# First attention in two passes of two batches, with the queries and keys of a head as seven half products

## The reference, cut to what matters

```python
projected = jnp.einsum('bsd,ed->bse', x, w_in)          # x is the layer norm here
q, k, v = jnp.split(projected.reshape(b, s, 16, 3 * 128), 3, axis=-1)
scores = jnp.einsum('bqhd,bkhd->bhqk', q, k) * (1.0 / np.sqrt(128))
scores = jnp.where(causal_mask, scores, -jnp.inf)
out = jnp.einsum('bhqk,bkhd->bqhd', jax.nn.softmax(scores), v)
return jnp.einsum('bse,de->bsd', out.reshape(b, s, 16 * 128), w_out)
```

## Time and profile before

| | whole span | 480 to 540 us (first attention) |
|---|---|---|
| PE busy | 2306.0 us (94%) | 60.00 of 60 us |
| DVE busy | 1661.4 us (68%) | 36.40 |
| ACT busy | 1120.8 us (46%) | 27.42 |
| POOL busy | 611.0 us (25%) | 9.98 |
| granted TensorE clock (1.00 is 2.4 GHz) | 0.983 | 1.00 |

### The profile page before, as it was taken

One profiled execution on the slowest core, in us unless ns is written; L12 is line 12 of the kernel. 1 busy time (PEld: TensorE's weight loads), 2 busy tenths in 40 slices (PEclk: granted clock), 3 DMA queues, 4 the chain that ended last, 5 costly groups with the idle time before them and its releaser, 6 DMA issues. The chain is left out here.

```text
span 2440.7 us, 40753 instructions
## 1 busy us (share of the span) xinstructions
PE 2306.0 (94%) x12966; PEld 1979.7 (81%) x12966; DVE 1661.4 (68%) x3852; ACT 1120.8 (46%) x2649; POOL 611.0 (25%) x497
## 2 busy tenths in 40 slices
PE   6999999999999999978999779999999999889997
PEld 5889898989898988856788558888888888767886
DVE  7555555564655554577666748998998999975666
ACT  3444444343434443443333435665666566542334
POOL 1111111110111111135121323333333333234223
PEclk9999999999999999989999889999999999999998
DMA  4524333334242424224885200000000000017866
GB/s 167 180 93 141 132 109 136 132 104 168 92 179 92 154 104 143 105 86 184 295 284 189 77 19 1 19 19 0 18 18 18 0 18 18 18 53 272 278 237 233
DMA packets 101006, 279.83 MB, mean 115 GB/s; under 512 B 8840, under 2 KB 11272, under 8 KB 95264
## 3 DMA queue, kind: packets, MB, share of 16 engines
q1 hardware_dynamic: 80032, 222.81, 25.9%
q0 software_dynamic: 11360, 37.76, 4.0%
q10 hardware_dynamic: 9504, 17.85, 2.2%
HBM read 133.40 MB, written 144.98 MB: 114 GB/s over the span
## 5 line engine op out<-in xcount | busy, mean ns | idle before, releaser
L74 PE MATMUL bank<-xT_hi,w_hi 128*128 128x512 f32 x864 | 349.7, 405 | 18.6 <-POOL w_lo L700 5.7
L76 PE MATMUL bank<-xT_hi,w_lo 128*128 128x512 f32 x864 | 343.3, 397 | 0.0
L75 PE MATMUL bank<-xT_lo,w_hi 128*128 128x512 f32 x864 | 343.3, 397 | 0.0
L619 DVE TENSOR_TENSOR hq_lo<-bank,hq_hi 128x512 fp32r<-128x512 f32 (+1 forms) x256 | 157.1, 624 | 251.5 <-ACT hq_hi L555 104.7
L609 DVE SCALAR_TENSOR_TENSOR x<-bank,inv,x 128x512 f32<-128x512 f32 x256 | 182.0, 748 | 170.6 <-PE bank L76 170.6
L74 PE MATMUL bank<-wo_hi,hq_hi 128*128 128x512 f32 x576 | 232.3, 403 | 15.3 <-DVE x L1050 13.7
L75 PE MATMUL bank<-wo_lo,hq_hi 128*128 128x512 f32 x576 | 226.7, 393 | 0.0
L76 PE MATMUL bank<-wo_hi,hq_lo 128*128 128x512 f32 x576 | 226.5, 393 | 0.0
L74 PEld LDWEIGHTS bank<-xT_hi,w_hi 128*128 128x128 f32 x864 | 166.2, 192 | 54.8 <-DVE xT_lo L178 9.8
L76 PEld LDWEIGHTS bank<-xT_hi,w_lo 128*128 128x128 f32 x864 | 165.5, 192 | 35.6
L75 PEld LDWEIGHTS bank<-xT_lo,w_hi 128*128 128x128 f32 x864 | 165.8, 192 | 33.9
(11 more groups left out here) (297 smaller groups left out, 6309.4 us busy)
## 6 DMA issues: line engine op xcount, KB each, us to landing
sorted_x<-blank SPq DMA_DIRECT2D x48, 1584.0 KB, 10.9
arena<-split_w SPq DMA_DIRECT2D x32, 1024.0 KB, 5.9
split_w<-arena SPq DMA_DIRECT2D x48, 512.0 KB, 3.0
raw<-dram_wr SPq DMA_DIRECT2D x24, 512.0 KB, 5.9
w_raw<-dram_wa SPq DMA_DIRECT2D x16, 512.0 KB, 3.8
arrived<-routed_y SPq DMA_DIRECT2D x8, 1024.0 KB, 8.2
w_raw<-dram_wb SPq DMA_DIRECT2D x8, 768.0 KB, 4.4
row_pt_hi<-sorted_x ACTq DMA_DIRECT2D x22, 264.0 KB, 4.2
```

Of the source, the lines that this page charges most:

```text
L74: nc.tensor.matmul(out, hi, mov_hi, start=first, stop=False)
L75: nc.tensor.matmul(out, hi, mov_lo, start=False, stop=False)
L76: return nc.tensor.matmul(out, lo, mov_hi, start=False, stop=last)
L619: return nc.vector.tensor_tensor(out, bank, hi.bitcast(F32), ALU.subtract).then_inc(done, 1)
```

## The change

The order becomes two passes: pass 0 does batches 0 and 1 for all 16 heads, pass 1 does batches 2 and 3. There are still 64 steps, now s = 2·(16·pass + head) + i. All weights are loaded and split in each pass, so twice.

For heads 1 to 14 of each pass the queries and keys of both batches are one 2x2 block product (batch x half of the features, times half of the features x query or key weights), done by Strassen's scheme in Winograd's form: seven half products (M1 to M7, each two k, 6 matmuls) and not eight. The operands that are sums are made beside: POOL sums weights (T1 to T4, four 128x256 operations per head, then split like weights), and once per pass, in head 0, POOL and DVE sum the inputs, stored where the other pair of batches has its xT. The results are summed by DVE out of PSUM, seven 128x512 operations per head, into SBUF buffers; the rounded part and the remainder of q and k are then taken from those buffers. Heads 0 and 15 keep whole queries and keys; head 0 holds the input sums, and head 15 holds the layer norm of the next pair of batches (pass 0: batches 2 and 3 for this attention; pass 1: batches 0 and 1 for the mixture of experts), whose tiles POOL scales. In pass 1 the statistics of batches 0 and 1 stand at the end of step i = 0 of head 14. The core of the diff, first the half product and one of its users, and PE's order in heads 1 to 14 (even i = 0, even i = 1, odd i = 0, odd i = 1) and in head 15:

```diff
+    def half_product(bank, weights, j, inputs, begin=True, close=True):
+        for k in range(2):
+            at = slice((2 * j + k) * DH, (2 * j + k + 1) * DH)
+            last = product(nc, m.bank[bank][:, :], weights[HI][:, at], weights[LO][:, at],
+                           inputs[HI][:, k, :], inputs[LO][:, k, :], begin and k == 0, close and k == 1)
+        return last
...
+    def m5(g, h):
+        pe.wait_ge(a.folded, folds_to(g, h, FOLD_U2))
...
+        half_product(4, m.wt, T1, sums(g, 1)).then_inc(a.folding, 1)
...
+        elif not edge(h) and not odd and i == 0:
+            m5(g, h)
+            outputs((0, 1))
+            m2(g, h)
+            turned()
+            m3(g, h)
+            outputs((2, 3))
+            attended()
...
+            project_v(g, h, i, 0)
...
+            project_v(g, h, i, 1)
+        elif not edge(h) and not odd:
...
+            m7(g, h)
+            outputs((0, 1))
...
+            m4(g, h)
+            turned()
+            outputs((2, 3))
+            pe.wait_ge(a.folded, folds_to(g, h, FOLD_Q1))
+            project_v(g, h, i, 0)
+            attended()
+            project_v(g, h, i, 1)
+        elif not edge(h) and i == 0:
+            pe.wait_ge(a.v_lo, values_count(g, h, odd, 1) - 2)
+            m1(g, h)
+            outputs((0, 1))
...
+            m6(g, h)
+            turned()
+            m5(g, h)
+            m2(g, h)
+            m3(g, h)
+            outputs((2, 3))
+            attended()
+        elif not edge(h):
+            m7(g, h)
+            outputs((0, 1))
+            m4(g, h)
+            turned()
+            outputs((2, 3))
...
+            m1(g, h + 1)
+            attended()
+            m6(g, h + 1)
...
+            norm_tiles(g, i, v, (0, 1))
+            whole_q(g, h, odd, i)
+            norm_tiles_out(g, i, (0, 1))
+            outputs((0, 1))
+            turned()
+            norm_tiles(g, i, v, (2, 3))
+            whole_k(g, h, odd, i)
+            attended()
+            norm_tiles_out(g, i, (2, 3))
+            outputs((2, 3))
```

ACT: odd heads, i = 0 (in front of it stand the late weights, the exponentials and `split_wo`), and the end of a step:

```diff
+            if odd:
+                first_product(g, h, s, 0)
...
+            probs_hi(u)
+            if odd:
+                query_hi(g, h, s, i)
+            key_hi(g, h, s, i)
...
+            if not odd and i:
+                sums_hi(g)
         if n1:
...
+            output_hi(u)
+        if new and not odd:
+            values_hi(g, h, i)
+        if new and i:
+            if g == 0:
+                prepare(h)
```

DVE, after `mask_and_max`: odd heads i = 0, heads 1 to 14 i = 1, the tail of head 0, and the end of a step:

```diff
+            add((0, 1))
+            with_m6(g, h, s)
+            probs_lo(u, (0,))
+            with_m5(g, h, s)
+            probs_lo(u, (1, 2))
+            first_query(g, h, s)
+            first_key(g, h, s)
+            query_lo(g, h, s, i)
+            key_lo(g, h, s, i)
+            add((2, 3))
...
+            second_key(g, h, s)
+            add((0, 1))
+            second_query(g, h, s)
+            probs_lo(u)
+            key_lo(g, h, s, i)
+            query_lo(g, h, s, i)
+            add((2, 3))
...
+            key_lo(g, h, s, i)
...
+            if i:
+                input_sums(g)
+            add((2, 3))
...
+            output_lo(u)
+        if new and not edge(h) and odd and i:
+            with_m6(g, h + 1, s + 1)
+        if new and edge(h) and not odd and i:
+            sums_lo(g)
+        if new and not odd:
+            values_lo(g, h, i)
+        if new and g == 1 and i == 0 and isinstance(h, int) and h == H - 2:
+            measure()
```

POOL, one head:

```diff
+        if not edge(h):
+            rest_late(g, h)
...
+        rest_wo(g, h, odd)
+        if edge(h) and odd:
+            late_rows(g, 0, (2, 3))
+            late_rows(g, 1, (0, 1))
+        if coming and not edge(coming[1]):
+            weight_sums(*coming)
...
+            rest_ahead(*coming)
+        if edge(h) and not odd:
+            third_sum(g)
+        if odd and coming:
+            rest_vw(*coming)
...
+            prepare(h)
```

More of the change, by code:

```diff
@@ L352, in project_k @@
[L352 to L364, removed]
-            for k in range(KD):
[L366 to L369, removed]
@@ L435, in steps @@
[L435 to L454, removed]
-        else:
[L456 to L459, removed]
-    if mla and part == 2:
-        act.wait_ge(a.wo_loaded, 16 * h + 16)
-        if again:
-            act.wait_ge(a.combined, h)
-        nc.scalar.activation(m.w[HI][:, dst[0]:dst[1]], m.wo_raw[:, 0:D], ACT.Copy).then_inc(a.w_hi, 1)
-    else:
-        nc.scalar.activation(m.w[HI][:, dst[0]:dst[1]], m.w_raw[:, src[0]:src[1]], ACT.Copy).then_inc(a.w_hi, 1)
@@ L469, in attend_scalar, with norm_tiles @@
[L469 to L481 removed]
+    def norm_tiles(g, i, v, tiles):
+        r, batch = late_batch(g, i)
+        pe.wait_ge(a.y_added, NT * v + (2 if tiles[0] else 0))
+        for t in tiles:
+            norm_tile_tensor(nc, pe, m, n, r, batch, t)
@@ new lines, in steps, with split_pass_weights @@
+    def steps(g, pair, odd):
+        h = 2 * pair + odd
+        begins = g == 0 and isinstance(h, int) and h == 0
+        for i in range(2):
+            step(g, h, odd, i, not begins or i > 0, not begins, hook=first if begins else nothing)
+    over_heads(pe, steps)
+    step(PASSES, 0, 0, 0, True, True, new=False)
+    step(PASSES, 0, 0, 1, False, True, new=False)
+def split_pass_weights(nc, act, m, a, g, h, part):
+    hh = H * g + h
+    if part == "first":
+        act.wait_ge(a.w_loaded, 16 * hh + 16)
+        src, dst = m.w_raw[:, 0:512], m.w[HI][:, 0:512]
+    if part == "second":
+        src, dst = m.w_raw[:, 512:1024], m.w[HI][:, 512:1024]
+    if part == "early":
+        act.wait_ge(a.t_summed, HEAD_PARTS * folded(g, h) + 2)
+        src, dst = m.t12, m.wt[HI][:, 0:512]
+    if part == "late":
+        act.wait_ge(a.t_summed, HEAD_PARTS * folded(g, h) + 4)
+        src, dst = m.t34, m.wt[HI][:, 512:1024]
+    nc.scalar.activation(dst, src, ACT.Copy).then_inc(a.w_hi, 1)
@@ L581, in steps @@
[L581 to L596 removed]
+            nc.scalar.activation(m.pt_hi[:, dst:dst + cols], m.bank[src][:, 0:cols], ACT.Copy).then_inc(a.pt_hi, 1)
@@ new lines, in steps, with attend_vector, mask_and_max @@
+    def steps(g, pair, odd):
+        h = 2 * pair + odd
+        begins = g == 0 and isinstance(h, int) and h == 0
+        for i in range(2):
+            step(g, pair, h, odd, i, not begins or i > 0, hook=first if begins else nothing)
+    split_pass_weights(nc, act, m, a, 0, 0, "first")
+    split_pass_weights(nc, act, m, a, 0, 0, "second")
+    split_vw(0, 0)
+    over_heads(act, steps)
+    step(PASSES, 0, 0, 0, 0, True, new=False)
+def attend_vector(nc, dve, m, n, a, first=nothing, measure=nothing):
+    def mask_and_max(u, slot):
@@ new lines, in step, with steps @@
+        if n1:
+            output_lo(u)
[5 more added lines that the diff above has]
+            values_lo(g, h, i)
+        if new and g == 1 and i == 0 and isinstance(h, int) and h == H - 2:
+            measure()
+        hook(i, 3)
+    def steps(g, pair, odd):
+        h = 2 * pair + odd
+        begins = g == 0 and isinstance(h, int) and h == 0
+        for i in range(2):
+            step(g, h, odd, i, not begins or i > 0, not begins, hook=first if begins else nothing)
```

1004 lines of the change are left out of this document (595 added, 409 removed).

## The result

The changed kernel takes 2429.4 us (median of four runs, 2427.7 to 2432.2), the kernel before 2442.7 beside it (2441.1 to 2443.3): ratio 0.9946, with a 95% interval of 0.9934 to 0.9958. That is 13.3 us faster; forecast were 2428 and a gain of 15. The profiled span fell from 2440.7 to 2428.1.

A forecast was written before the change was run, and what follows sets the result against it. PE was taken to bound the attention, so PE work removed is time gained. -38.2 + 5 + 21 - 5.6 + 14 + 9.5 - 5.9 - 14.9 = -15.1 us gave a median of 2428 us, range 2402 to 2452.

The forecast's parts named there:

- seven products and small stalls: Heads 1 to 14, both passes: 28 blocks each lose 1.365 us on PE, -38.2; SBUF-port meetings give back +5.
- input sums, both passes: Head 0 of each pass: values queue behind input sums, PE stalls 8.5 and 7.0 plus 2.7 clock each, +21 us.
- head 0 without norms: Head 0 no longer holds the norms of batches 2 and 3: 19.8 us against 14.2, -5.6 us.
- head 15, both passes: Head 15: 3.2 us of transposes and 3.8 us waiting for POOL's tiles, twice 7.0, +14 us (8 to 16).
- statistics: Pass 1, head 14: two batches' statistics delay the next mask; 6.8 us stall and 2.7 clock, +9.5 us (6.8 to 11).
- stall before the last step: Statistics and norms leave the last steps, so the stall of 3.18 us goes with its clock: -5.9 us.
- end: Last projection's end to the experts' first matmul: 33.0 us before, 18.1 after, -14.9 us (2 either way).
- Small stalls of the port: Odd heads: q and k residuals meet POOL at SBUF; 0.35 us per pair of heads taken, +5 us (0 to 14).
- the rival: Shared SBUF port decides: both residuals of each odd step meet POOL, 34 us in place of 5, 2457 us; chance 0.17.
- in two parts too short for the clock: Head 15: PE's 3.8 us wait for POOL's rows comes in two parts, so no clock loss was counted.

The follow-up runs named there:

- The experiment: Changed kernel with POOL making rows 2 and 3 of the first batch ahead of the output weights' subtraction in head 15 (rows first): 2423.4 us.
- the run with the values first: Changed kernel with head 0's values' copies and residuals ahead of the last two copies and residuals of the input sums: 2413.1 us.
- the run with the statistics split: Changed kernel with pass 1's statistics in head 14 done as batch 0 in the first step and batch 1 in the second: 2422.6 us.
- less of M4: Changed kernel with M4 as one matmul, not six, in heads 1 to 14: 2409.1 us.
- M4 twice: Changed kernel with M4 issued twice in heads 1 to 14, the second copy overwriting the first: 2469.5 us.

## Why the prediction was right, and which of its terms were not

The forecast's mechanism held: the products' time is gained almost in full, and most of it is spent at the edges. That 2428 stood so near 2429.4 is partly luck: its terms were off by up to 4.5 us each, and the errors nearly cancel. Measured up to the experts' first matmul (1073.69, before 1086.74):

| step | predicted | measured |
|---|---|---|
| seven products and small stalls | -38.2 + 5 | -37.7 (remainder of this table; 14 x 2.65 = 37.1 by the pairs) |
| input sums, both passes | +21 | +21.1 (9.2 + 1.6 and 8.3 + 1.95) |
| head 0 without norms | -5.6 | -5.2 |
| head 15, both passes | +14 | +18.1 |
| statistics | +9.5 | +8.1 |
| stall before the last step | -5.9 | -5.9 |
| end | -14.9 | -12.7 |
| start | not named | +1.2 |
| sum | -15.1 | -13.05 |

**Small stalls of the port.** Mis-sized: +5 against about 1 (a pair gained 64.22 - 61.57 = 2.65 us of 2.73). The meetings are there, and each is as dear as the step said: a residual of 0.68 takes up to 1.78 us. The slack was about as named, too. What failed is the 0.35 us of each pair that was to get past it: by the rows of one pair each odd step had one meeting's worth, 0.37 + 0.55 us in i = 0 and 1.10 in i = 1, and that stayed inside. q's and k's residuals of i = 0 ended at 266.2, 0.3 us ahead of the scores, and M1 + M6 in i = 1 ended 1.0 us ahead of M5. The rule of the Trainium skill (SBUF — State Buffer, section "SBUF: two separate sides") agrees with the rows: POOL's third sum, begun 0.04 us behind DVE's, took 3.45 us and not 2.41, 1.04 longer where 1.19 of DVE's operation were left, while DVE's own row kept its 1.23. But a toll on an engine is one on the path only where the hand-over has no slack; the rival needed 1.4 us a pair and had about 0.1.

**Input sums.** Right in size and place, down to ACT's copy that waits for POOL. Here the port's toll did reach PE, as the step had it: in front of M1 the three residuals lost about 3 us to POOL in pass 0 and 4 in pass 1. The idle clock cost less per pass than 2.7 (1.6 and 1.95), the stalls a little more.

**Head 15.** The step was right about whose wait it is: 1.67 + 1.38 us for POOL's rows. It failed at "in two parts too short for the clock": the granted clock was 0.79 in that stretch and the keys took 1.6 us more, 1.2 in pass 1. The experiment got back both together. But the clock is no fixed price there: in four of the thirteen head 15s of these profiles with the same two waits it cost nothing (last section).

**Statistics.** 6.6 + 1.5 in place of 6.8 + 2.7; the clock again was mis-sized. **End.** The last softmax, one DVE residual and the additions were the waits, as named, but 1.4 + 0.85 + 1.5 + 0.2 us of them stand in a stretch with a clock of 0.86, which the step had not counted: 20.3 us, not 18.1. The clock is 1.5 of these 2.2: in the run with the rows first the same waits stand in a full clock, and the end takes 18.75. **Start.** The first weights' subtraction came at 7.8 us of wait where it had been 5.7. This differs from run to run (6.2 to 7.8 in the profiles of changed kernels). It too is a queue: ACT had rounded these weights by 15.7 us, but on POOL a copy that the code holds until all of the small loads are there stands ahead of their subtraction, and it started at 19.82 us, before at 19.10. Why it starts later is open.

## What to carry to other kernels

Where the profile shows that one engine never waits in a long stretch, work taken from it counts in full until the first hand-over runs out of slack; write that slack down in us, and measure it by taking away a little more. The cost of a restructuring sits where the pattern begins and ends: look there at what stands ahead of the awaited instruction in each in-order queue, for some 34 us of this kernel came back through order alone, with the same work. A stall of 1 to 2 us on PE can be dearer than it looks, since the matmuls behind it may run at the lower clock: here it cost 1.2 to 2.3 us more behind most such stalls and nothing behind others, and that alone can make a run look better or worse than its edit.

## What the runs showed of the hardware that was not expected

Behind two waits of PE of 1.7 and 1.4 us, with four transposes between them, the clock could fall: the stretch from 508 to 516 us had a granted clock of 0.79, and twelve matmuls took 4.42 and not 2.84 us. Behind a single wait of 1.81 us, in the run with the values first, twelve took 4.42 as well. With one wait of 0.73 us in head 15 they took 2.83. But the same two waits did not always do it. In the run with the statistics split, head 15 of pass 0 has them, and its keys take 513.80 - 510.96 = 2.84 us; the last line is its stretch, with a granted clock of 1.00:

```profile
508.54 0.63 PE L214 MATMUL bank<-ident,xn 128*128 128x128 f32 x4 [1.67 <-DVE x L823]
510.55 0.66 PE L214 MATMUL bank<-ident,xn 128*128 128x128 f32 x4 [1.38 <-POOL xn L1092]
510.96 0.48 PE L74 MATMUL bank<-xT_hi,w_hi 128*128 128x512 f32 x1
...
513.80 0.39 PE L74 MATMUL bank<-pt_hi,hq_hi 128*128 128x512 f32 x1
508.50:516.50 8.00, 6.58 (x36) 5.63 (x37) 2.65 (x5) 1.79 (x3) 6.12 (x3) 1.00 0.95 342
```

So do pass 1's in the runs with the values first, with less of M4 and with M4 twice (2.84, 2.83 and 2.85 us). No run here shows what decides.

A DVE operation with two SBUF inputs that met a POOL operation in SBUF waited for it, and the other way round. Beside the case above, a residual of 1024 columns on DVE took 3.31 us behind POOL's third sum in the run with the values first, and 2.03 us in its last place, where POOL was subtracting weights:

```profile
54.49 3.31 DVE L838 TENSOR_TENSOR xT_lo<-xT_lo,xT_hi 128x1024 fp32r<-128x1024 f32 x1
...
66.44 2.03 DVE L838 TENSOR_TENSOR xT_lo<-xT_lo,xT_hi 128x1024 fp32r<-128x1024 f32 x1
```

A 1024-column sum that met nothing took 1.23 us, which is what the prediction had estimated.
